# Four graph layers in one kernel: six node slots per edge tile instead of seven, and layer 0's one-hots built four tiles at a time

## The reference, cut to what matters

```python
x = _layernorm(x + _L0(x, edge_index, ...))   # mean of x[src] per dst, two 128x128 matrices
x = _layernorm(x + _L1(x, edge_attr, ...))    # relu(x[src] @ W1a + edge_attr @ W1b + b1), mean per dst, then W2, W3, W4
x = _layernorm(x + _L2(x, edge_attr, ...))    # h = x_comb + segment_sum(x_comb[src], dst), two matrices
x = _layernorm(x + _L3(x, ...))               # GAT: 4 heads, softmax over the edges of each dst
```

## Time and profile before

| | |
|---|---|
| median of three runs | 6451.55 us |
| span of the profiled execution, first to last instruction | 5707.4 us |
| median less span | 744.2 us |
| PE (TensorE matmul) busy | 4531.6 us, 79% |
| PEld (TensorE weight load) busy | 3717.3 us, 65% |
| DVE (VectorE) busy | 2795.5 us, 49% |
| ACT (ScalarE) busy | 1993.7 us, 35% |
| POOL (GpSimd) busy | 3118.8 us, 55% |
| mean granted TensorE clock | 0.890 |

### The profile page before, as it was taken

One profiled execution on the slowest core, in us unless ns is written; L12 is line 12 of the kernel. 1 busy time (PEld: TensorE's weight loads), 2 busy tenths in 40 slices (PEclk: granted clock), 3 DMA queues, 4 the chain that ended last, 5 costly groups with the idle time before them and its releaser, 6 DMA issues.

```text
span 5707.4 us, 76723 instructions
## 1 busy us (share of the span) xinstructions
PE 4531.6 (79%) x25589; PEld 3717.3 (65%) x25589; DVE 2795.5 (49%) x10327; ACT 1993.7 (35%) x4098; POOL 3118.8 (55%) x3336
## 2 busy tenths in 40 slices
PE   6999998999999999999998999644545544544544
PEld 5999997667677777767768999634444444444444
DVE  8999996333333333433345444333443443443444
ACT  5888886222222222222224555211111121111112
POOL 0000002777777777777770000377777777777775
PEclk9999999999999999999999999777777777677777
DMA  6777777777767777777766777422222222222221
GB/s 153 170 167 165 165 168 178 210 212 210 210 210 211 209 212 208 212 208 212 209 189 191 243 244 246 123 55 56 56 56 56 56 56 56 56 56 56 57 56 43
DMA packets 479979, 843.08 MB, mean 148 GB/s; under 512 B 73951, under 2 KB 302474, under 8 KB 468074
## 3 DMA queue, kind: packets, MB, share of 16 engines
q0 software_dynamic: 141920, 462.69, 32.3%
q1 hardware_dynamic: 323562, 365.74, 21.0%
q10 hardware_dynamic: 14112, 9.74, 0.5%
HBM read 682.70 MB, written 155.18 MB: 147 GB/s over the span
## 4 chain that ended last, share of the span: by engine, by line
PE 49%; POOL 26%; issue 10%; DMA 7%; DVE 6%; ACT 1%; ACTq 0%; POOLq 0%; DVEq 0%
POOL ring L536 26%; PE bank L1196 9%; PE bank L1028 9%; PE bank L681 8%; PE bank L1015 7%; PE bank L662 4%; DMA ring<-ptab,src 4%; DMA ring<-htab,src 2%; PE bank L1478 2%; PE bank L1514 2%; PE bank L1507 1%; PE bank L576 1%; DVE ring L1405 1%; DMA atab<-at 1%; PE bank L1485 1%
## 5 line engine op out<-in xcount | busy, mean ns | idle before, releaser
L536 POOL DMA_INDIRECT ring<-htab,src x1612 | 1527.4, 947 | 503.1 <-issue 472.2
L536 POOL DMA_INDIRECT ring<-ptab,src x1612 | 1526.8, 947 | 498.6 <-issue 440.7
L1028 PE MATMUL bank<-ring,oh 128*126 128x384 f32 x3224 | 1213.7, 488 | 0.0
L982 DVE TENSOR_TENSOR ring<-bank,ring 128x512 f32<-128x512 f32 x806 | 529.9, 685 | 1231.8 <-DMA ring<-ptab,src 1227.7
L1015 PE MATMUL bank<-w1e,ea 128*128 128x256 f32 x3224 | 845.7, 385 | 46.2 <-DVE ring L982 37.3
L998 ACT ACTIVATE ring<-ring 128x1024 f32<-128x1024 f32 x403 | 425.6, 1056 | 1252.8 <-DVE ring L982 1252.8
L1015 PEld LDWEIGHTS bank<-w1e,ea 128*128 128x128 f32 x3224 | 601.1, 190 | 354.0 <-DVE ring L982 119.8
L681 PE MATMUL bank<-xhl,at 128*126 128x258 f32 x4410 | 815.3, 325 | 1.0 <-ACT at L642 1.0
L1514 PE MATMUL bank<-ring,oh 128*126 128x132 f32 x3224 | 589.8, 316 | 244.9 <-DVE ring L1405 244.3
L642 ACT ACTIVATE at<-bank 128x343 fp32r<-128x343 f32 x1612 | 731.2, 489 | 140.7 <-PE bank L662 61.6
L1028 PEld LDWEIGHTS bank<-ring,oh 128*126 128x126 f32 x3224 | 589.8, 188 | 199.8
(11 more groups left out here) (268 smaller groups left out, 5298.0 us busy)
## 6 DMA issues: line engine op xcount, KB each, us to landing
atab<-at POOLq DMA_DIRECT2D x90, 1543.5 KB, 9.6
ring<-ea_r SPq DMA_DIRECT2D x403, 256.0 KB, 4.0
ea<-ea_t SPq DMA_DIRECT2D x403, 256.0 KB, 3.1
adjb<-atab SPq DMA_DIRECT2D x180, 535.5 KB, 4.7
adjb<-atab SPq DMA_DIRECT2D x90, 472.5 KB, 4.2
ring<-ptab,src POOLq DMA_INDIRECT x1612, 3.5
ring<-htab,src POOLq DMA_INDIRECT x1612, 2.5
ptab<-pO ACTq DMA_DIRECT2D x49, 128.0 KB, 4.6
```

The costliest lines, as they stand in the source:

```text
L536: return e.indirect_dma_start(o, None, table, bass.IndirectOffsetOnAxis(ap=src[:, t:t + 1], axis=0))
L982: e.tensor_tensor(group1(gi, m % 2), MLP[m % 3][:, :].rearrange("p (g f) -> p g f", g=2), group1(gi, m % 2), ALU.add).then_inc(s_edge, 1)
L1028: e.matmul(SUM[s % 2][0:SL, 0:384], slots_of(s, i), rv1[:, t // G % NR1, t % G, :], start=i == 0, stop=t == END[s]).then_inc(s_sum1, 1)
```

## The change

S becomes 6, so GT = 21 and SL = 126 as before; a group has up to 21 tiles, and `groups` ends one early where it would touch a third block. By the planner's numbers there are then 78 groups: 70 of 21 tiles, seven of 17 to 19 and a last one of 12. The pairs of a group and a block fall from 173 to 152. The helper `where(p)` gives group, tile in the group and size for a place, and the loops use it. Layer 0's adjacency has 6 x 49 = 294 columns. Its one-hots are made for G = 4 tiles by one `tensor_tensor` each, with the tile as the innermost dimension, and TensorE reads one tile with a step of four bf16 elements (8 bytes), both as weights and as the moving operand. There are NQ = 3 buffers of four tiles. The codes are made in five segments (64 tiles, then four of 387), all by place 32. Layer 3's ring is four groups of 21 = 84 tiles; layer 1's stays at 9 x 4. The first part of the diff below changes constants; the rest is what runs in layer 0 and the waits of layer 3.

```diff
-S = 7
+S = 6
-    NRING = 27
-    NR1 = NRING * HROW // 384
+    NR1 = 9
+    NR3 = 4
+    RING = max(NR3 * GT * HROW, NR1 * G * 384)
-    NU = 8
+    NQ = 3
+    SEGS = [0, 64] + [64 + -(-(NT - 64) * k // 4) for k in range(1, 5)]
...
-        iob = sb("iob", [P, P], BF)
-        ioc = sb("ioc", [P, S * NB], BF)
+        iob = sb("iob", [P, P, G], BF)
+        ioc = sb("ioc", [P, S * NB, G], BF)
...
             def dense_hots(e, d, q):
+
                 if q == 0:
                     codes(e, d, 0)
-                elif q % GT == GT // 2 and q // GT + 1 < NS:
-                    codes(e, d, q // GT + 1)
-                if q < NT:
-                    s, i = q // GT, q % GT
-                    if i == 0:
-                        e.wait_ge(d.code, 5 * s + 5)
-                    if q >= NU:
-                        e.wait_ge(d.adj, q - NU + 1)
-                    e.tensor_scalar(hotU[:, q % NU, :], iob[:, :], low[:, s % 2, i:i + 1], None, ALU.is_equal).then_inc(
-                        d.hot, 1)
-                    e.tensor_scalar(hotV[:, q % NU, 0:S * NB], ioc[:, :], code[:, s % 2, i:i + 1], None,
-                                    ALU.is_equal).then_inc(d.hot, 1)
+                if q % 8 == 0 and 1 <= q // 8 < len(SEGS) - 1:
+                    codes(e, d, q // 8)
+                if q < NT and q % G == 0:
+                    k = q // G
+                    e.wait_ge(d.code, 5 * next(i for i in range(1, len(SEGS)) if q < SEGS[i]))
+                    if k >= NQ:
+                        e.wait_ge(d.adj, G * (k - NQ + 1))
+                    for o, i, c, n in ((hotU, iob, low, P), (hotV, ioc, code, S * NB)):
+                        e.tensor_tensor(o[:, k % NQ, :, :], i[:, :, :], c[:, q:q + G].unsqueeze(1).broadcast_to([P, n, G]),
+                                        ALU.is_equal).then_inc(d.hot, 1)
...
-                    e.wait_ge(d.hot, 2 * q + 2)
+                    e.wait_ge(d.hot, 2 * (q // G) + 2)
-                    e.matmul(ADJ[q % 3][:, 0:S * NB], hotU[:, q % NU, :], hotV[:, q % NU, 0:S * NB], start=True,
+                    e.matmul(ADJ[q % 3][:, 0:S * NB], hotU[:, q // G % NQ, :, q % G], hotV[:, q // G % NQ, :, q % G], start=True,
...
             def pool3(e):
                 e.wait_ge(s_htab, 16 * NB)
-                for gi in range(NG):
-                    if gi >= NRING:
-                        e.wait_ge(s_sum3, G * (gi - NRING + 1))
-                    for j in range(G):
-                        t = gi * G + j
-                        gather(e, rv3[:, t % (NRING * G), :], htab[:, :], t).then_inc(row_sem(3, gi)[0], 16)
+                for s in range(NS):
+                    for i in range(SIZE[s]):
+                        if s >= NR3 and i % G == 0:
+                            e.wait_ge(s_sum3, START[s - NR3] + min(i + G, SIZE[s - NR3]))
+                        gather(e, rv3[:, s % NR3 * GT + i, :], htab[:, :], START[s] + i).then_inc(landed3(s)[0], 16)
```

More of the change, by code:

```diff
@@ L25 @@
 YW = 258
-Dense = namedtuple("Dense", "code hot adj count low blank sum kept node add clear")
+Dense = namedtuple("Dense", "code hot adj count low sum kept node add clear")
 def plan(n_nodes, n_edges, n_rand):
@@ L48, in groups @@
 def groups(nt, first, last):
-    ns = -(-nt // GT)
-    return ns, [first[GT * s] for s in range(ns)], [last[min(GT * s + GT, nt) - 1] for s in range(ns)]
+    start, t = [], 0
+    while t < nt:
+        start.append(t)
+        t = next((u for u in range(t + 1, min(t + GT, nt)) if last[u] - first[start[-1]] > 1), min(t + GT, nt))
+    size = [b - a for a, b in zip(start, start[1:] + [nt])]
+    return start, size, [first[a] for a in start], [last[a + n - 1] for a, n in zip(start, size)]
 def weave(n_places, opens, n_steps):
@@ L139, in sem, with where @@
             return ctx.enter_context(nc.semaphore(name))
+        def where(p):
+            if p < NT:
+                return GROUP[p], p - START[GROUP[p]], SIZE[GROUP[p]]
+            return NS + (p - NT) // GT, (p - NT) % GT, GT
         def wide(s):
@@ L229, in build @@
         s_prep_v, s_prep_t, s_prep_a = (sem(f"s_prep_{n}") for n in "vta")
-        s_row = [sem(f"s_row{i}") for i in range(NRING)]
+        s_row = [sem(f"s_row{i}") for i in range(NR1)]
+        s_row3 = [sem(f"s_row3_{i}") for i in range(NR3)]
         s_ea = [sem(f"s_ea{i}") for i in range(NR1)]
@@ L520, in expected, with landed1, landed3 @@
             hbf = hflat.bitcast(BF)
-            hotU = hbf[:, 0:NU * P].rearrange("p (n c) -> p n c", n=NU)
-            hotV = hbf[:, NU * P:NU * (P + 352)].rearrange("p (n c) -> p n c", n=NU)
+            hotU = hbf[:, 0:NQ * G * P].rearrange("p (n c g) -> p n c g", n=NQ, g=G)
+            hotV = hbf[:, NQ * G * P:NQ * G * (P + S * NB)].rearrange("p (n c g) -> p n c g", n=NQ, g=G)
+            low, code = (hbf[:, 2 * WHOT + i * NT:2 * WHOT + (i + 1) * NT] for i in range(2))
             ADJ = bank[1], bank[4], bank[5]
             AT = tuple(at0[:, i, :].rearrange("p (b c) -> p b c", c=SL) for i in range(2))
-            rv3 = ring[:, :].rearrange("p (t f) -> p t f", f=HROW)
-            def row_sem(layer, gi):
-                i = gi % (NR1 if layer == 1 else NRING)
-                if layer == 1:
-                    return s_row[i], 64 * (gi // NR1 + 1)
-                before = len(range(i, NG, NR1)) if i < NR1 else 0
-                return s_row[i], 64 * (before + gi // NRING + 1)
+            rv3 = ring[:, 0:NR3 * GT * HROW].rearrange("p (t f) -> p t f", f=HROW)
+            def landed1(gi):
+                return s_row[gi % NR1], 64 * (gi // NR1 + 1)
+            def landed3(s):
+                return s_row3[s % NR3], 16 * sum(SIZE[w] for w in range(s % NR3, s + 1, NR3))
             def gather(e, o, table, t):
@@ L673, in dense_sums @@
                         e.wait_ge(d.count, END[g] + 1)
-                        if g == NS - 1 and END[g] - GT * g + 1 < GT:
-                            e.wait_ge(d.blank, 1)
                         if g >= 2:
                             e.wait_ge(d.kept, g - 1)
-                    for h in range(NB * i // GT, NB * (i + 1) // GT):
+                    for h in range(NB * i // n, NB * (i + 1) // n):
                         if g == 0 and h % CB == 0:
@@ L1186, in tensor2 @@
                 for q in range(N2):
-                    g, i = q // GT, q % GT
-                    for h in range(NB * i // GT, NB * (i + 1) // GT) if g < NS else ():
+                    g, i, n = where(q)
+                    for h in range(NB * i // n, NB * (i + 1) // n) if g < NS else ():
                         u, c = 3 * g + h // THIRD, h % THIRD
@@ L1213, in expected, with odd_from @@
                                                    "most", "logit_in", "logit", "exp", "weigh"))
-            def tiles(s):
-                return END[s] - GT * s + 1
+            CW = [sum(-(-n // CH) for n in SIZE[0:s]) for s in range(NS + 1)]
+            def odd_from(s):
+                return START[s] % 2
             def rows3(s, n):
-                o = GT * s % (NRING * G)
+                o = s % NR3 * GT
                 return rv3[:, o:o + n, :]
@@ L1288, in front3 @@
                 elif k == 12:
-                    m = tiles(s)
+                    m = SIZE[s]
                     e.wait_ge(s_logit_in, s + 1)
@@ L1821, in lay_out @@
     out["nxtT"] = np.ascontiguousarray(dst[2:].reshape(nt, P).T)
-    ns, sb0, _ = groups(nt, first, last)
-    head = np.full(ns * GT, npad, np.int32)
-    head[:nt] = dst[1:-1].reshape(nt, P)[:, 0]
-    out["dhead"] = head[:nt]
+    start, size, sb0, _ = groups(nt, first, last)
+    head = np.ascontiguousarray(dst[1:-1].reshape(nt, P)[:, 0])
+    out["dhead"] = head
+    slots = np.full((len(start), GT), npad, np.int32)
+    for g, (a0, n) in enumerate(zip(start, size)):
+        slots[g, :n] = head[a0:a0 + n]
     ends = np.zeros((4, -(-nt // P) * P), np.int32)
-    ends[0, :nt], ends[1, :nt] = head[:nt], dst[1:-1].reshape(nt, P)[:, -1]
+    ends[0, :nt], ends[1, :nt] = head, dst[1:-1].reshape(nt, P)[:, -1]
     ends[2, :nt] = [P * b for b in first]
```

135 lines of the change are left out of this document (63 added, 72 removed).

## The result

The changed kernel takes **6509.81 us** (median of 4 runs, 6506.98 to 6524.22), the kernel before beside it 6451.64: a ratio of 1.0095, 95% interval 1.0080 to 1.0109. It is 58 us slower; 6288 was forecast.

What follows compares the result with a forecast made beforehand. TensorE was taken to bound layers 0 and 2, GpSimd's gathers layers 1 and 3. Layer 0 -91.2, layer 2 -74.7 and edges +2 gave -164 us, from 6451.55 to 6288 us; range 6255 to 6410.

Steps and rivals of the forecast that it cites:

- The strided read: TensorE's adjacency in layer 0, read at a step of 8 bytes: taken to cost nothing; upper bound +197 us at half rate.
- Rival 1: The strided moving operand runs at half rate in layer 0's adjacency: 6473 us; chance 0.11 with its like.
- Sum matmuls, adds, columns: TensorE: fewer sums -70.6 us (layer 0), -70.0 (layer 2); adds to nodes -4.7 in each; 49 fewer adjacency columns -32.9 us.
- the coupling: Layer 0: ScalarE, paced close to TensorE, hardly regains what it loses in tails: 0.15 us a group, +12 us, bounds 0 and 35.
- the +5 us for the start: Layer 0's start: sums wait for 21 tiles instead of 18, with codes segments made in between: +5 us, bounds 0 and 10.
- VectorE's comparisons: Layer 0's one-hots, two wide instructions for four tiles: 1.02 us, 0.255 a tile against 0.38; VectorE gets off the limit.
- Rival 2: VectorE's two-source comparison stays at 1.04 ns an element and VectorE becomes the bound: 6428 us; chance 0.07.
- The store: Layer 0's matrix store: no longer than before and 12 fewer; off the path unless it lands after 10.6 us.
- Rival 3: ScalarE and the store become the bound in layer 0: 6310 to 6335 us; chance 0.14.
- Layers 1 and 3: Gathers stay 1612 in each, one every 1.25 us, GpSimd never waiting for the ring: no gain, +1 us at layer 3's end.
- the sign that was named for being wrong: GpSimd's gathers showing gaps over 0.30 us in layer 3 of the profile after.
- the margin of 34 us in the ring: Layer 3, 84 tiles: a group's sums end at 71 us, its places are wanted again at 105 us, so 34 are left.

Runs made afterwards that it cites:

- t1_tile: Changed kernel, six slots and groups kept, but each tile's two one-hots made by tensor_scalar and contiguous: 6314.23 us, ratio 0.9785.
- s1_pair: Changed kernel with one-hots made for two tiles at a time, so TensorE reads at a step of 4 bytes: 6313.78 us, ratio 0.9775.
- b0_before: The kernel before, unchanged, profiled once more in a single run: 6455.1 us, span 6450.2 us.
- `y` runs: Two kernels with layer 3's ring of 72 tiles and groups of 18, with landing signalling exchanged between old and new loops: 5719.60 and 5699.45 us.
- y2: Six slots, groups up to 18, one-hots by tile, ring of 72, a landing semaphore for each four tiles: 5699.45 us, 0.9957 of the kernel before.
- y1: Kernel before with layer 3's ring of 72 tiles and one landing semaphore for each group instead of each four tiles: 5719.60 us, ratio 0.9994.

## Why the prediction was wrong, point by point

- **The strided read** is the step that failed. "I take nothing, the nearer row being one factor of two away." The rows on either side of a doubling don't say on which side its knee is: 4 bytes, the step of f32, is the last one of the four measured that is nearly free. The moving operand measured 0.26 us for 0.14, the whole 0.27; the term was +194 us (1004.5 - 810.0) where 0 was put, and +14 of it, at 0.009 us a tile, came from the weight load, which was put at nothing too. The upper bound of +197, for the moving operand alone, was near: that operand brought 181 us. The Trainium skill's cacheline note (SBUF — State Buffer, section "Door 1: The DMA port swizzle"), by which two hits on a 16-byte line suffice for full bandwidth, does not hold for TensorE's moving operand here: a step of 8 bytes has two hits, and 294 columns took 0.26 us instead of 0.14. The measurement decides.
- **Rival 1** was what happened: layer 0 at -91 + 197 - 12 = +94 us, measured +95. That they meet within 1 us is in part luck, since the bound was 16 us high for the moving operand and the weight load's 14 us were missing. It gave 6473 us; the 37 us to 6509.81 are mostly layer 3's 42.
- **Sum matmuls, adds, columns**: right. Without the stride (`t1_tile`), layer 0 goes from 909.6 to 810.0 us, -99.6 for -91.2. TensorE is busy there for 493.21 of 500 us, so it loses 1.4%, 11 us of 810, and lost 0.7%, 6 us, before: by that estimate the coupling cost 5 us, not 12, in a kernel whose comparisons are by tile. With wide comparisons (`s1_pair`) layer 0 is 95.0 us shorter than before. Of the +5 us for the start only the first part can be told: the first sum begins 13.9 us after the first adjacency, 12.3 in `b0_before`. Layer 2: -74.3 for -74.7.
- **VectorE's comparisons**: right. 0.34 us from start to start for 512 elements; the one of 1176 lasts 0.76 us, of which 0.09 overlap with the next as in the row before it:

```profile
502.42 0.43 DVE L636 TENSOR_TENSOR hs<-iob,hs 128x512 bf16<-128x512 bf16 x1 [0.99 <-PE bank L667]
502.76 0.76 DVE L636 TENSOR_TENSOR hs<-ioc,hs 128x1176 bf16<-128x1176 bf16 x1
```

0.34 + 0.67 = 1.01 us for four tiles, 1.02 forecast. Rival 2 is excluded. The Trainium skill's table (VectorE: DVE Perf Modes, section "The perf-mode tier table"), which caps a bf16 `tensor_tensor` at two elements per cycle and one in f32 at one, agrees, with one operand repeated over the columns by a zero step. The two widths give (0.67 - 0.34) / 664 = 0.50 ns an element and 0.09 us fixed, where 0.52 and 0.07 were taken; the earlier trace rows have one width of f32 alone, so that the split into 1.04 ns and 0.07 us was an estimate.
- **The store**: off the path, landing 9.5 us after its issue, 9.6 before:

```profile
DMA to landing us min/median/max: 9.0/9.5/11.4
```

Rival 3 got no chance to act, with TensorE busy throughout; in `t1_tile`, where the adjacency is fast again and TensorE was busy for 493.21 of 500 us, it didn't either.
- **Layers 1 and 3**: the mechanism "a gather every 1.25 us and never a wait" is that of the one execution shown, and of the `y` runs. In the timed runs GpSimd pauses for ring places, and the sign that was named for being wrong, gaps over 0.30 us in layer 3, came true. Layer 1 took the same time in both kernels all the same. Layer 3 grew by 42 us, where +1 was forecast; the margin of 34 us in the ring was reckoned from the wrong kind of execution. Even in the kind that was shown the term isn't borne out: `y2`, six slots with groups of 18, took 18 us more there than `y1`. Leaving 744 us "around the span" unexplained was an error of reading: the median less the span was a warning that the profile and the times didn't belong together, and it should have widened the range by what layers with gathers might do.
- **Open**: what makes layer 3 longer, and what makes two kinds of executions. Ring length, group size and the signalling were each varied, and none explains the 42 us; identical code spreads by 48, by 21 within one set of runs. What holds it up is seen, not explained. In the timeline of the changed kernel (TensorE, then GpSimd, VectorE and ScalarE):

```profile
4645.70 2.07 PE L1481 MATMUL bank<-rT,sel 84*126 84x128 f32 x8 [4.33 <-issue]
...
4650.24 1.09 PE L1517 MATMUL bank<-ring,oh 128*126 128x132 f32 x4
...
4654.78 0.95 POOL L552 DMA_INDIRECT ring<-htab,src  x1 [0.30 <-issue]
4659.23 0.69 DVE L1265 TENSOR_TENSOR tops<-bank,away 126x512 f32<-126x512 f32 x1 [13.29 <-remote]
4659.29 0.38 ACT L1447 ACTIVATE o2T<-bank 128x252 f32<-128x252 f32 x1 [13.65 <-remote]
...
4662.10 0.94 POOL L552 DMA_INDIRECT ring<-htab,src  x1 [6.37 <-PE bank L1517]
```

TensorE's L1481, for which VectorE's L1265 waits, is done at 4647.8; VectorE goes on 11.4 us later, and ScalarE at the same moment. It isn't the gathers' rows: of the DMA engines' share of time from 4655 to 4660, in 40 slices, nothing is left after 4656.8, though both engines resume only at 4659.2:

```profile
DMA  0991000000094500000000000000000000000000
```

The chain of the whole span puts 24% on "another core or an unknown queue", and 23% in `b0_before`, so this marks the kind of execution and not the change. The name is to be taken with care, for the traces of this kind are incomplete in the layers with gathers: of the 25792 signals by which layer 3's gathers tell that they have landed (16 each), the changed kernel's trace holds 4813 and `b0_before`'s 4769, that of the profile of before 25768. A wait whose signal wasn't recorded can't be put down to anybody. Whether the missing records and the longer time have one cause, no run here shows.

## What to carry to other kernels

Before a layout is changed to save an engine work, look at every reader of it: on TensorE the bf16 moving operand whose columns lie 8 bytes apart cost about twice the time here (0.26 us for 0.14), while two tiles interleaved (4 bytes, 0.15 us) cost 5 us in the whole of layer 0, and still let VectorE compare two tiles at once. Where only a bound is known, and it is as large as the whole gain, measure by one interleaved operand before building the change; here the versions with two tiles or one (0.9728 and 0.9735 with a ring of 63 tiles, 0.9715 for the best, which those intervals don't tell apart) have the gain that was forecast. And where the median and the profiled span differ by much more than usual (744 us here, 1.5 to 5.2 us in the profiles whose own time is known), suspect that the profile is of another kind of execution, and count on it only for the stages that both share.

## What the runs showed of the hardware that was not expected

- A bf16 matmul of 294 columns, moving operand and weights both strided: 0.14, 0.15, 0.27 and 0.56 us from start to start at steps of 2, 4, 8 and 16 bytes, on a clock of 1.00. Loading its weights of 128 columns: 96, 98, 114 and 146 ns.
- Two kinds of executions of one kernel on one core, steady within a set of runs and both seen on one chip: 5723.01 us in one set, 6451 to 6471 in the others. Only stages with indirect gathers differ: 1612 gathers in layer 1 take 2015 to 2020 us in the one, 2354 to 2374 in the others.
- In executions of about 6450 us, the same instructions of layer 3 took 2433 to 2481 us in six kernels that differ only elsewhere. The rows of its gathers had landed within 3.5 us in either kind of execution.
- A shorter ring in layer 3 was slightly faster there: 72 tiles instead of 108 gave 0.9967 (0.9955 to 0.9980) of the kernel before.
